# Record scatters three deep instead of two, shared rows prefetched one a step, and the last additions moved to GpSimd

## The chip, the cores and the metric

The kernel runs on one core of one Trainium2 chip. The metric is the device time of one execution in microseconds (us). Engines are named as the profile names them: PE (TensorE), DVE (VectorE), ACT (ScalarE), POOL (GpSimd) and SP (SyncE, which here only issues DMAs).

## What is computed

A transformer block in float32 on x of shape (4, 1024, 256): a cross attention of 16 heads against 64 context rows per batch, then a mixture of 8 experts with 2 of them chosen for each token, and one shared expert that every token passes.

```python
x = x + xattn(layernorm(x), ctx_768, Wq, Wk, Wv, Wo, bo)      # 16 heads of 64, softmax over 64 keys
xf = layernorm(x).reshape(-1, 256)                            # 4096 tokens
scores = softmax(xf @ gate_w.T); _, idx = top_k(scores + gate_b, 2)
w = take_along_axis(scores, idx)                              # 2 of 8 experts per token
expert(x) = silu((x @ w1 + b1) * (x @ w3 + b3)) @ w2 + b2     # 256 -> 352 -> 256
y = sum over the two chosen experts of w * expert_e(xf)
x = x + y + shared_expert(xf)
```

## The kernel before

The 4096 tokens are 32 tiles of 128 (NT = 32). After a setup of some 67 us the work runs in two phases, both software pipelined: in each step every engine works on another tile, and the order on an engine is the order of the code. All waits are semaphores written by hand.

**Attention phase**, `tile_step(s)`, s = 0 to 37. Tile t is loaded as `xin` at s = t-3 (SP, L445), its statistics are taken by DVE at s = t-2 (L999), and its scores, softmax and output follow on PE, ACT, DVE and POOL. At t+4 its sum with the residual `x2` is stored to `acc0` in DRAM (L453), at t+5 the normalised rows `xn2` to `xn2_scratch` (L449). DVE also chooses experts for tiles 0 to 7 and 8 to 15 in steps 14 to 19 and 22 to 27. In between SP loads the expert weights (L488 to L495). At step 20 SP also loads eight tiles of `xn2` rows (`shared_x`, L516) that the next phase begins with.

**Record scatters.** Each token gets, for each of its two experts, a slot in a table in DRAM (`slots_scratch`), where tokens of one expert stand together. POOL writes the table with 64 indirect DMAs (`scatter_record`, L649), two per tile, one record of 8 bytes for each of 128 tokens. Each waits for an earlier one by semaphore: `scat_out[k]`, k being the first or the second choice, so a scatter waits for the one two back. 22 of the 64 are issued during steps 20 to 30, one tile a step; the other 42 come behind the attention phase.

**Expert phase**, `unit_step(s)`, s = 0 to 106. It walks 103 units of 128 rows: shared tiles 0 to 19, then 71 routed units (`NU`) whose rows POOL gathers by the table (`gather`, L698) and whose results it adds into `acc0` or `acc1` (`scatter_add`, L705), then shared tiles 20 to 31. In step s PE does the second product of unit s-4 (`Y`), transposes the rows of s and the hidden values of s-3 (L1391, L1399) and does the first product of s-1. DVE computes low parts (`uxTl` L1124, `hTl` L1129), adds the bias (`uv` L1142) and multiplies (`hid<-uv` L1145); ACT copies out of PSUM and does silu. Before the first gather SP waits for all record scatters (L537) and then loads one piece of the table for each unit (L532), and POOL waits for that piece.

**The end.** Results of shared tiles 20 to 31 (units 91 to 102) go from PSUM to `zrow` (ACT, L897). When all scatter-adds have landed, SP loads both accumulators into `sums` in eight quads of four tiles (L551). DVE adds the two halves of one quad in each of the last eight steps, and `zrow` to the last three quads, between its other work (L1155, L1158, L1161); SP stores each quad (L555):

```python
both = [sums[:, i, q, :, :].rearrange("p a d -> p (a d)") for i in range(2)]
dve.wait_ge(sums_in[q], 32)
```

## Time and profile before

| | |
|---|---|
| time, median of 3 runs | 759.71 us (757.81 to 766.28) |
| the profiled execution's own time | 761.5 us |
| its span in the trace | 759.8 us |
| PE busy | 681.3 us, 90% of the span |
| DVE busy | 531.0 us, 70% |
| POOL busy | 409.8 us, 54% |
| ACT busy | 402.2 us, 53% |
| mean granted PE clock | 0.961 of full |

Busy time is a sum over stages with different limits, so it does not say what an edit is worth: that is read from the waits and from the stretch in which the edit lies. All times in the text are us from the start of the span.

### The profile page before, as it was taken

The numbers are of one execution on the slowest core, as the hardware profiler recorded it, in microseconds if no ns is written. First come the engines' busy times: TensorE is split into PE (matmuls) and PEld (weight loads), VectorE is DVE, ScalarE is ACT, GpSimd is POOL, SyncE is SP. The second block draws the span as 40 slices with busy tenths as digits, with TensorE's granted clock in tenths as the row PEclk, the third lists the DMA queues.
The fourth block names the chain that finished last, engine by engine and source line by source line (L and its number), as shares of the span: only waits on it lengthen the run. The fifth ranks groups of instructions, "written<-read, shape, count | busy, mean of one in ns | idle before, by whom it ended". The sixth has DMA issues, their size and how long they took to land.

```text
span 759.8 us, 16832 instructions
## 1 busy us (share of the span) xinstructions
PE 681.3 (90%) x4645; PEld 636.6 (84%) x4646; DVE 531.0 (70%) x1085; ACT 402.2 (53%) x1311; POOL 409.8 (54%) x506
## 2 busy tenths in 40 slices
PE   4997799999998999967899079999999999999995
PEld 3775599998897889857899079999999999999994
DVE  4766688788976887658889036666666666666677
ACT  3875778787766667746533024434443444344342
POOL 5343475544566677433454435777677777766200
PEclk9989999999999999988999679999999999999998
DMA  8201222235436664316221024454444444455495
GB/s 240 77 0 42 91 70 78 84 109 162 131 93 151 122 122 92 101 59 177 67 64 34 2 64 63 74 72 74 76 72 69 76 74 71 70 96 105 94 392 229
DMA packets 71508, 74.83 MB, mean 98 GB/s; under 512 B 21130, under 2 KB 65012, under 8 KB 71444
## 3 DMA queue, kind: packets, MB, share of 16 engines
q1 hardware_dynamic: 51940, 50.51, 24.3%
q0 software_dynamic: 15760, 18.96, 15.3%
q10 hardware_dynamic: 3744, 4.59, 1.7%
q8 instruction: 30, 0.49, 0.3%
q14 instruction: 34, 0.28, 0.2%
HBM read 47.22 MB, written 26.81 MB: 97 GB/s over the span
## 4 chain that ended last, share of the span: by engine, by line
PE 74%; DMA 13%; DVE 5%; issue 4%; ACT 2%; POOL 2%; SPq 1%; ACTq 0%; POOLq 0%; DVEq 0%
PE ps L1221 61%; DMA slots_scratch<-record,slot 11%; PE ps L1399 4%; PE ps L1318 3%; PE ps L1391 2%; PE ps L1295 1%; DMA wq_sb<-in_L_xattn_Wq 1%; PE ps L1308 1%; POOL slots_scratch L649 1%; ACT prob L763 1%; DMA xin<-in_x 1%; DVE hmax L1008 1%; SPq L516 1%; PE ps L1346 1%; DVE sums L1158 0%
## 5 line engine op out<-in xcount | busy, mean ns | idle before, releaser
L705 POOL DMA_INDIRECT acc_scratch<-yrow,slots x71 | 112.0, 1578 | 71.0 <-ACT yrow L889 70.7
L889 ACT ACTIVATE yrow<-ps,slots 128x256 f32<-128x256 f32 x71 | 33.7, 475 | 148.2 <-PE ps L1221 131.4
L1221 PE MATMUL ps<-AU,xTh 128*128 128x512 f32 x256 | 96.9, 423 | 9.1 <-DVE xTl L1021 9.1
L1221 PE MATMUL ps<-AU,pTh 128*128 128x256 f32 x512 | 100.2, 288 | 0.0
L1221 PE MATMUL ps<-w13h,uxTh 128*128 x284 | 97.7, 344 | 0.0
L1142 DVE TENSOR_TENSOR uv<-ps,b 128x704 f32<-128x704 f32 x71 | 63.3, 892 | 47.7 <-PE ps L1221 46.5
L649 POOL DMA_INDIRECT slots_scratch<-record,slot x64 | 66.1, 1033 | 56.2 <-DMA slots_scratch<-record,slot 46.8
L1221 PE MATMUL ps<-w13h,uxTl 128*128 x284 | 91.6, 322 | 0.0
L1221 PE MATMUL ps<-w13l,uxTh 128*128 x284 | 91.2, 321 | 0.0
L1124 DVE TENSOR_TENSOR uxTl<-ps,uxTh 128x256 fp32r<-128x256 f32 x103 | 43.6, 423 | 65.7 <-ACT uxTh L903 65.3
L698 POOL DMA_INDIRECT xrow<-xn_scratch,slots x71 | 69.8, 983 | 26.0 <-issue 20.1
L1221 PEld LDWEIGHTS ps<-AU,pTh 128*128 128x128 f32 x512 | 81.4, 189 | 0.0
L763 ACT ACTIVATE prob<-ps,nmax 128x64 f32<-128x64 f32 x256 | 76.3, 338 | 6.0 <-DVE nmax L1011 6.0
L1221 PE MATMUL ps<-AU,pTl 128*128 128x256 f32 x256 | 72.2, 282 | 0.0
L604 POOL TENSOR_TENSOR prob<-prob,hinv 128x1024 f32<-128x1024 f32 x32 | 60.9, 1904 | 20.5 <-DVE hinv L990 20.4
L1221 PEld LDWEIGHTS ps<-AU,xTh 128*128 128x128 f32 x256 | 49.8, 195 | 19.1 <-DVE xTl L1021 10.1
L1391 PE MATMUL ps<-ident,xrow 128*128 128x128 f32 x206 | 40.5, 279 | 26.5 <-DMA xrow<-xn_scratch,slots 22.9
L1221 PE MATMUL ps<-w2h,hTh 128*128 x213 | 63.0, 296 | 0.0
L1221 PE MATMUL ps<-w2l,hTh 128*128 x213 | 60.4, 283 | 0.0
L1221 PE MATMUL ps<-w2h,hTl 128*128 x213 | 60.1, 282 | 0.0
L763 ACT ACTIVATION_READ_ACCUMULATOR prob<-ps,nmax 128x1 f32 x256 | 59.3, 232 | 0.0
L1129 DVE TENSOR_TENSOR hTl<-ps,hTh 128x384 fp32r<-128x384 f32 x103 | 57.3, 556 | 0.3 <-ACT hTh L908 0.3
(237 smaller groups left out, 2009.9 us busy)
## 6 DMA issues: line engine op xcount, KB each, us to landing
sums<-acc_scratch SPq DMA_DIRECT2D x16, 512.0 KB, 10.9
w_raw<-in_L_ffn_w SPq DMA_DIRECT2D x16, 352.0 KB, 4.0
xin<-in_x SPq DMA_DIRECT2D x32, 128.0 KB
xres<-in_x SPq DMA_DIRECT2D x32, 128.0 KB
acc_scratch<-x SPq DMA_DIRECT2D x32, 128.0 KB
xn_scratch<-xn SPq DMA_DIRECT2D x32, 128.0 KB
xrow<-xn_scratch SPq DMA_DIRECT2D x32, 128.0 KB
out_x<-sums SPq DMA_DIRECT2D x8, 512.0 KB, 2.8
```

The source lines that it names most:

```text
L604: pool.tensor_tensor(heads, heads, hinv[:, p, :].unsqueeze(2).to_broadcast([P, HEADS, NK]), ALU.mult).then_inc(norm_ok, 1)
L649: pool.indirect_dma_start(slots_dram, bass.IndirectOffsetOnAxis(ap=slot[:, k, t:t + 1], axis=0), record[:, t, k, :], None).then_inc(scat_o ...
L698: pool.indirect_dma_start(xrow[:, m, :], None, xn2_dram, bass.IndirectOffsetOnAxis(ap=slots[:, u, 0:1], axis=0)).then_inc(gather_in[m], 16)
L705: pool.indirect_dma_start(acc_dram[u % 2], bass.IndirectOffsetOnAxis(ap=slots[:, u, 0:1], axis=0), yrow[:, m % YRING, :], None, compute_op ...
L763: act.activation(prob[:, p, h * NK:(h + 1) * NK], ps[:, s_bank(p) + h // 8, h % 8 * NK:(h % 8 + 1) * NK], ACT.Exp, bias=nmax[:, p, h - HS: ...
L889: act.activation(yrow[:, y, :], ps[:, 6 + m % 2, 0:D], ACT.Copy, scale=slots[:, bass.ds(u, 1), 1].bitcast(F32)).then_inc(y_ok, 1)
L1124: dve.tensor_tensor(uxTl[:, p, :], ps[:, 0, 0:D], f32(uxTh[:, p, :]), ALU.subtract).then_inc(uxTl_ok, 1)
L1129: dve.tensor_tensor(hTl[:, :], ps[:, 5, 0:H3], f32(hTh[:, :]), ALU.subtract).then_inc(hTl_ok, 1)
L1142: dve.tensor_tensor(uv[:, :, :], ps[:, 1 + 2 * p:3 + 2 * p, 0:H], bias, ALU.add).then_inc(bias_ok, 1)
L1221: last = pe.matmul(out, stationary(k, a), moving(k, b), start=(k == 0 and i == 0), stop=(k == n - 1 and i == len(PARTS) - 1 and not more))
L1391: last = pe.transpose(ps[:, 0, k * P:(k + 1) * P], xrow[:, m, k * P:(k + 1) * P], ident[:, :])
L1399: last = pe.transpose(ps[:, 5, k * P:(k + 1) * P], hid[:, p, k * P:(k + 1) * P], ident[:, :])
```

## The change

It has five parts. (1) The 64 record scatters use three semaphores in turn (`FLIGHT = 3`): scatter n waits for n-3 and no more for n-2. SP waits for all three. Two semaphores more are needed for this and for the new end; they come from `raw2_in`, which now counts two experts on one semaphore, so that ACT's first copy of a pair waits for both. (2) The eight loads of shared rows leave step 20 and stand one each in steps 24 to 31, behind the expert weights of the step. (3) POOL, behind its last scatter-add, adds the two halves of all eight quads; DVE's eight additions of this kind go. (4) DVE adds `zrow` to quads 5 and 6 in steps 102 and 103. (5) For the last quad (units 99 to 102) ACT copies nothing out; in steps 103 to 106 DVE adds each tile's PSUM result to `sums` directly, ahead of its other work of the step, and SP stores it tile by tile.

```diff
--- before.py
+++ after.py
@@ -50,10 +50,12 @@
     NU = TOP * NT + E - 1
     RING = 8
     YRING = 4
+    FLIGHT = 3
     QUAD = 4
     NA = 20
     NB = NT - NA
     R0, R1 = NA, NA + NU
+    RD = R1 + NB - QUAD
     GROUPS = ((0, 8), (8, 16))
     REST = (16, NT)
     NREST = NT - 16
@@ -329,11 +331,11 @@
         rank_copied = sem("rank_copied")
         empty_raw = sem("empty_raw")
         empty_ok = sem("empty_ok")
-        scat_out = [sem(f"scat_out{k}") for k in range(TOP)]
+        scat_out = [sem(f"scat_out{i}") for i in range(FLIGHT)]
         slots_in = [sem(f"slots_in{i}") for i in range(RING)]
 
         raw13_in = [sem(f"raw13_in{e}") for e in range(E)]
-        raw2_in = [sem(f"raw2_in{e}") for e in range(E)]
+        raw2_in = [sem(f"raw2_in{i}") for i in range(E // 2)]
         w13_hi = sem("w13_hi")
         w2_hi = sem("w2_hi")
         w_lo = sem("w_lo")
@@ -358,8 +360,9 @@
         shared_row_out = [sem(f"shared_row_out{i}") for i in range(YRING)]
         z_row_ok = sem("z_row_ok")
         sums_in = [sem(f"sums_in{q}") for q in range(NT // QUAD)]
-        sums_ok = sem("sums_ok")
+        both_ok = sem("both_ok")
         out_ok = sem("out_ok")
+        last_ok = sem("last_ok")
         all_out = sem("all_out")
         y_out = sems("y_out")
         NALL = NT + NU
@@ -490,9 +493,9 @@
 
             def load_w2(e):
                 sp.wait_ge(pad2_zero, 1 if e < EARLY2 else 2)
-                sp.dma_start(w2_raw[:, e, 0:KH - 1, :], w2[e, 0:(KH - 1) * P, :].rearrange("(c p) d -> p c d", p=P)).then_inc(raw2_in[e], 16)
-                sp.dma_start(w2_raw[0:HR, e, KH - 1, :], w2[e, (KH - 1) * P:H, :]).then_inc(raw2_in[e], 16)
-                sp.dma_start(w2_raw[HR:HR + 1, e, KH - 1, :], b2[e, :].rearrange("(a d) -> a d", a=1)).then_inc(raw2_in[e], 16)
+                sp.dma_start(w2_raw[:, e, 0:KH - 1, :], w2[e, 0:(KH - 1) * P, :].rearrange("(c p) d -> p c d", p=P)).then_inc(raw2_in[e // 2], 16)
+                sp.dma_start(w2_raw[0:HR, e, KH - 1, :], w2[e, (KH - 1) * P:H, :]).then_inc(raw2_in[e // 2], 16)
+                sp.dma_start(w2_raw[HR:HR + 1, e, KH - 1, :], b2[e, :].rearrange("(a d) -> a d", a=1)).then_inc(raw2_in[e // 2], 16)
 
             def begin_step(s, par):
                 tile_step(s, par)
@@ -504,11 +507,10 @@
                     load_w2(s - 24)
                 if s in (31, 32):
                     load_w2(s - 25)
-                if s == 20:
+                if 24 <= s < 24 + RING:
                     for half in xn2_out:
                         sp.wait_ge(half, 16 * RING // 2)
-                    for t in range(RING):
-                        shared_x(t)
+                    shared_x(s - 24)
 
             def shared_x(t):
                 m, i = t % RING, shared_tile(t)
@@ -534,8 +536,8 @@
             for t in range(RING, NA):
                 shared_x(t)
             sp.wait_ge(eid_ok, 1)
-            for half in scat_out:
-                sp.wait_ge(half, 16 * NT)
+            for i in range(FLIGHT):
+                sp.wait_ge(scat_out[i], 16 * len(range(i, TOP * NT, FLIGHT)))
             for u in range(NU):
                 unit_slots(u)
             for t in range(R1, NALL):
@@ -549,11 +551,17 @@
                 b, j = divmod(q * QUAD, TPB)
                 for i in range(2):
                     sp.dma_start(sums[:, i, q, :, :], acc_tiles[i][:, b, j:j + QUAD, :]).then_inc(sums_in[q], 16)
-            for q in range(NT // QUAD):
+            for q in range(NT // QUAD - 1):
                 b, j = divmod(q * QUAD, TPB)
-                sp.wait_ge(out_ok, q + 1)
+                if q < NA // QUAD:
+                    sp.wait_ge(both_ok, q + 1)
+                else:
+                    sp.wait_ge(out_ok, q - NA // QUAD + 1)
                 sp.dma_start(out_tiles[:, b, j:j + QUAD, :], sums[:, 0, q, :, :]).then_inc(all_out, 16)
-            sp.wait_ge(all_out, 16 * (NT // QUAD))
+            for i in range(QUAD):
+                sp.wait_ge(last_ok, i + 1)
+                sp.dma_start(out_tiles[:, B - 1, TPB - QUAD + i, :], sums[:, 0, NT // QUAD - 1, i, :]).then_inc(all_out, 16)
+            sp.wait_ge(all_out, 16 * (NT // QUAD - 1 + QUAD))
 
 
         @block.gpsimd
@@ -645,9 +653,10 @@
                 return done
 
             def scatter_record(t, k):
-                wait(pool, scat_out[k], 16 * t)
+                n = TOP * t + k
+                wait(pool, scat_out[n % FLIGHT], 16 * (n // FLIGHT))
                 pool.indirect_dma_start(slots_dram, bass.IndirectOffsetOnAxis(ap=slot[:, k, t:t + 1], axis=0),
-                                        record[:, t, k, :], None).then_inc(scat_out[k], 16)
+                                        record[:, t, k, :], None).then_inc(scat_out[n % FLIGHT], 16)
 
             def begin_step(s, par):
                 tile_step(s, par)
@@ -714,6 +723,10 @@
                 scatter_add(u)
                 if u + ahead < NU:
                     gather(u + ahead)
+            for q in range(NT // QUAD):
+                both = [sums[:, i, q, :, :].rearrange("p a d -> p (a d)") for i in range(2)]
+                pool.wait_ge(sums_in[q], 32)
+                pool.tensor_tensor(both[0], both[0], both[1], ALU.add).then_inc(both_ok, 1)
 
 
         @block.scalar
@@ -858,7 +871,7 @@
                     act.activation(w13h[:, e, k, :], w13_raw[:, e, k, :], ACT.Copy).then_inc(w13_hi, 1)
 
             def high2(e):
-                act.wait_ge(raw2_in[e], 48)
+                act.wait_ge(raw2_in[e // 2], 96)
                 flat = [a[:, e, :, :].rearrange("p c d -> p (c d)") for a in (w2h, w2_raw)]
                 act.activation(flat[0], flat[1], ACT.Copy).then_inc(w2_hi, 1)
 
@@ -892,7 +905,7 @@
                         wait(act, Y_ok, t + 1)
                         wait(act, shared_row_out[y], 16 * (t // YRING))
                         act.activation(yrow[:, y, :], ps[:, 6 + m % 2, 0:D], ACT.Copy).then_inc(shared_row_ok, 1)
-                    else:
+                    elif t < RD:
                         wait(act, Y_ok, t + 1)
                         act.activation(zrow[:, t - R1, :], ps[:, 6 + m % 2, 0:D], ACT.Copy).then_inc(z_row_ok, 1)
                 t = s
@@ -1116,6 +1129,12 @@
             steps(NT, 2, 6, begin_step, begun=0)
 
             def unit_step(s, m, routed=None):
+                t = s - 4
+                if isinstance(t, int) and t >= RD:
+                    row = sums[:, 0, NT // QUAD - 1, t - RD, :]
+                    dve.wait_ge(both_ok, NT // QUAD)
+                    dve.wait_ge(Y_ok, t + 1)
+                    dve.tensor_tensor(row, ps[:, 6 + m % 2, 0:D], row, ALU.add).then_inc(last_ok, 1)
                 t = s
                 if has(t, NALL):
                     p = m % 2
@@ -1147,19 +1166,14 @@
                     low2(s - 5)
                 if isinstance(s, int) and 5 + E <= s < 5 + E + E - 3:
                     low13(s - 5 - E + 3)
-                q = s - NALL - LAG + NT // QUAD if isinstance(s, int) else -1
-                if q >= 0:
-                    both = [sums[:, i, q, :, :].rearrange("p a d -> p (a d)") for i in range(2)]
-                    dve.wait_ge(sums_in[q], 32)
-                    if q < NA // QUAD:
-                        dve.tensor_tensor(both[0], both[0], both[1], ALU.add).then_inc(out_ok, 1)
-                    else:
-                        z0 = (q - NA // QUAD) * QUAD
-                        dve.tensor_tensor(both[0], both[0], both[1], ALU.add).then_inc(sums_ok, 1)
-                        dve.wait_ge(sums_ok, q - NA // QUAD + 1)
-                        dve.wait_ge(z_row_ok, z0 + QUAD)
-                        dve.tensor_tensor(both[0], both[0], zrow[:, z0:z0 + QUAD, :].rearrange("p a d -> p (a d)"),
-                                          ALU.add).then_inc(out_ok, 1)
+                q = s - NALL + NT // QUAD - 2 if isinstance(s, int) else -1
+                if NA // QUAD <= q < NT // QUAD - 1:
+                    z0 = (q - NA // QUAD) * QUAD
+                    row = sums[:, 0, q, :, :].rearrange("p a d -> p (a d)")
+                    dve.wait_ge(both_ok, q + 1)
+                    dve.wait_ge(z_row_ok, z0 + QUAD)
+                    dve.tensor_tensor(row, row, zrow[:, z0:z0 + QUAD, :].rearrange("p a d -> p (a d)"),
+                                      ALU.add).then_inc(out_ok, 1)
 
             dve.wait_ge(lg_ok, NT)
             dve.wait_ge(O_ok, NT)
@@ -1374,8 +1388,10 @@
                         wait(pe, y_ok, t - 1 - R0)
                     elif t < R0 + 2:
                         wait(pe, shared_row_ok, t - 1)
+                    elif t < RD + 2:
+                        wait(pe, z_row_ok, t - 1 - R1)
                     else:
-                        wait(pe, z_row_ok, t - 1 - R1)
+                        wait(pe, last_ok, t - 1 - RD)
                     w2s = (w2h, w2l) if is_routed(t, routed) else (ws2h, ws2l)
                     product(ps[:, 6 + p, 0:D],
                             lambda k, part: (hTh, hTl)[part][:, k * P:(k + 1) * P],
```

SP's queue in the program's step 20, before: behind the loads of `xrow` stand the tile load of step 21 and all that follows.

```order
L516 DMA xrow<-xn_scratch 128x256 [waits xn2_out_odd,xn2_out_even]
L516 DMA xrow<-xn_scratch 128x256 x7
L445 DMA xin<-in_x 128x256 [waits xn_ok]
L449 DMA xn_scratch<-xn 128x256 [waits xn2_ok]
L453 DMA acc_scratch<-x 128x256 [waits x2_ok]
L457 DMA xres<-in_x 128x256 [waits x2_ok]
L488 DMA w_raw<-in_L_ffn_w 128x2x352 [waits O_ok]
L489 DMA w_raw<-in_L_ffn_w 128x2x352
```

SP's queue now in step 24, at the first of the eight places where one such load stands.

```order
L496 DMA w_raw<-in_L_ffn_w 128x2x256 [waits pad2_zero]
L497 DMA w_raw<-in_L_ffn_w 96x256
L498 DMA w_raw<-in_L_ffn_b 1x256
L518 DMA xrow<-xn_scratch 128x256 [waits xn2_out_odd,xn2_out_even]
L448 DMA xin<-in_x 128x256 [waits xn_ok]
L452 DMA xn_scratch<-xn 128x256 [waits xn2_ok]
L456 DMA acc_scratch<-x 128x256 [waits x2_ok]
L460 DMA xres<-in_x 128x256 [waits x2_ok]
```

The eight loads in a row are gone from the place ahead of `xin`, and one stands behind the three weight loads `w2` in each of steps 24 to 31 (from step 30 on partly without such loads). 

POOL's queue behind the attention phase, before: scatters of the fifth to the seventh tile left over.

```order
L649 DMA slots_scratch<-record,slot 33792x2 [waits scat_out0]
L649 DMA slots_scratch<-record,slot 33792x2 [waits scat_out1]
L649 DMA slots_scratch<-record,slot 33792x2 [waits scat_out0,slot_ok]
L649 DMA slots_scratch<-record,slot 33792x2 [waits scat_out1]
L649 DMA slots_scratch<-record,slot 33792x2 [waits scat_out0]
```

The same place now.

```order
L658 DMA slots_scratch<-record,slot 33792x2 [waits scat_out0]
L658 DMA slots_scratch<-record,slot 33792x2 [waits scat_out1]
L658 DMA slots_scratch<-record,slot 33792x2 [waits scat_out2,slot_ok]
L658 DMA slots_scratch<-record,slot 33792x2 [waits scat_out0]
L658 DMA slots_scratch<-record,slot 33792x2 [waits scat_out1]
```

The instructions are the same in number and order; only the semaphore that each waits on differs, with period three.

DVE's queue over the last steps, before (from step 103).

```order
L1129 TENSOR_TENSOR hTl<-ps,hTh 128x384 [waits Y_ok,hTh_ok]
L1142 TENSOR_TENSOR uv<-ps,bs 128x704 [waits z_ok,UV_ok]
L1145 TENSOR_TENSOR hid<-uv 128x352 [waits H_ok,bias_ok]
L1155 TENSOR_TENSOR sums<-sums 128x1024 [waits sums_in4]
L1129 TENSOR_TENSOR hTl<-ps,hTh 128x384 [waits Y_ok,hTh_ok]
L1158 TENSOR_TENSOR sums<-sums 128x1024 [waits sums_in5]
L1161 TENSOR_TENSOR sums<-sums,zrow 128x1024 [waits z_row_ok,sums_ok]
L1129 TENSOR_TENSOR hTl<-ps,hTh 128x384 [waits Y_ok,hTh_ok]
L1158 TENSOR_TENSOR sums<-sums 128x1024 [waits sums_in6]
L1161 TENSOR_TENSOR sums<-sums,zrow 128x1024 [waits z_row_ok,sums_ok]
L1158 TENSOR_TENSOR sums<-sums 128x1024 [waits sums_in7]
L1161 TENSOR_TENSOR sums<-sums,zrow 128x1024 [waits z_row_ok,sums_ok]
```

And now (from the end of step 102).

```order
L1175 TENSOR_TENSOR sums<-sums,zrow 128x1024 [waits z_row_ok,both_ok]
L1137 TENSOR_TENSOR sums<-ps,sums 128x256 [waits Y_ok,both_ok]
L1148 TENSOR_TENSOR hTl<-ps,hTh 128x384 [waits Y_ok,hTh_ok]
L1161 TENSOR_TENSOR uv<-ps,bs 128x704 [waits z_ok,UV_ok]
L1164 TENSOR_TENSOR hid<-uv 128x352 [waits H_ok,bias_ok]
L1175 TENSOR_TENSOR sums<-sums,zrow 128x1024 [waits z_row_ok,both_ok]
L1137 TENSOR_TENSOR sums<-ps,sums 128x256 [waits Y_ok,both_ok]
L1148 TENSOR_TENSOR hTl<-ps,hTh 128x384 [waits Y_ok,hTh_ok]
L1137 TENSOR_TENSOR sums<-ps,sums 128x256 [waits Y_ok,both_ok]
L1148 TENSOR_TENSOR hTl<-ps,hTh 128x384 [waits Y_ok,hTh_ok]
L1137 TENSOR_TENSOR sums<-ps,sums 128x256 [waits Y_ok,both_ok]
```

Behind each `hid<-uv` or `hTl` stood one or two additions of 1024 columns; two of these are left, and four additions of 256 columns out of PSUM have come, each ahead of the `hTl` of its step and each with a wait for `both_ok`, POOL's count.

## Rows read from the trace of the kernel before

**Rows 1.** The page, part 4: the chain that ended last.
```profile
PE ps L1221 61%; DMA slots_scratch<-record,slot 11%; PE ps L1399 4%; PE ps L1318 3%; PE ps L1391 2%; PE ps L1295 1%; DMA wq_sb<-in_L_xattn_Wq 1%; PE ps L1308 1%; POOL slots_scratch L649 1%; ACT prob L763 1%; DMA xin<-in_x 1%; DVE hmax L1008 1%; SPq L516 1%; PE ps L1346 1%; DVE sums L1158 0%
```

**Rows 2.** Waits of POOL, 330 to 440 us: total, times, longest.
```profile
POOL slots_scratch L649 <- DMA slots_scratch<-record,slot: 46.8, 29, 3.3
```

**Rows 3.** Timeline of POOL: start, duration, idle before and its releaser.
```profile
340.56 1.66 POOL L649 DMA_INDIRECT slots_scratch<-record,slot  x1 [0.41 <-issue]
...
415.46 0.96 POOL L649 DMA_INDIRECT slots_scratch<-record,slot  x1 [2.72 <-DMA slots_scratch<-record,slot]
...
419.00 0.96 POOL L649 DMA_INDIRECT slots_scratch<-record,slot  x1 [1.22 <-DMA slots_scratch<-record,slot]
...
433.98 0.96 POOL L649 DMA_INDIRECT slots_scratch<-record,slot  x1 [1.25 <-DMA slots_scratch<-record,slot]
439.40 0.99 POOL L698 DMA_INDIRECT xrow<-xn_scratch,slots  x1 [4.47 <-DMA slots<-slots_scratch]
```

**Rows 4.** Timeline of PE around its long wait.
```profile
442.55 0.69 PE L1391 MATMUL ps<-ident,xrow 128*128 128x128 f32 x2 [22.87 <-DMA xrow<-xn_scratch,slots]
...
448.59 0.38 PE L1391 MATMUL ps<-ident,xrow 128*128 128x128 f32 x2
...
452.12 0.38 PE L1391 MATMUL ps<-ident,xrow 128*128 128x128 f32 x2
```

**Rows 5.** Windows: busy time by engine, then PEclk, DMA share, GB/s.
```profile
340.00:360.00 20.00, 14.78 (x90) 13.42 (x89) 17.02 (x46) 11.37 (x21) 7.59 (x8) 0.78 0.61 173
434.00:445.00 11.00, 2.45 (x10) 2.46 (x11) 0.98 (x2) 1.26 (x3) 5.12 (x6) 0.50 0.20 43
```

**Rows 6.** Timeline of SP's DMA issues, steps 20 to 23.
```profile
220.64 4.96 SPq L516 DMA_DIRECT2D xrow<-xn_scratch  x8
225.65 0.43 SPq L445 DMA_DIRECT2D xin<-in_x  x1
...
227.00 0.32 SPq L453 DMA_DIRECT2D acc_scratch<-x  x1
...
246.38 0.33 SPq L453 DMA_DIRECT2D acc_scratch<-x  x1
...
254.38 0.33 SPq L453 DMA_DIRECT2D acc_scratch<-x  x1
```

**Rows 7.** Timeline of DVE in the step behind those issues.
```profile
231.27 0.43 DVE L999 BATCH_NORM_STATS2 st<-xin 128x6 f32<-128x256 f32 x1 [2.74 <-DMA xin<-in_x]
...
233.06 1.64 DVE L1011 TENSOR_SCALAR nmax<-hmax 128x8 f32<-128x8 f32 x1
...
250.62 0.30 DVE L1011 TENSOR_SCALAR nmax<-hmax 128x8 f32<-128x8 f32 x1
```

**Rows 8.** Timeline of POOL at the same two places.
```profile
233.27 1.40 POOL L660 MEMSET w_raw<- 128x1536 f32 x1
...
248.99 1.91 POOL L604 TENSOR_TENSOR prob<-prob,hinv 128x1024 f32<-128x1024 f32 x1 [0.70 <-DVE hinv L990]
```

**Rows 9.** POOL groups by shape: count, busy, mean ns.
```profile
L617 POOL TENSOR_TENSOR wol<-wo_raw,woh 128x256 fp32r<-128x256 f32 x8 | 5.8, 728 | 0.0
...
L671 POOL TENSOR_TENSOR ws2l<-ws,ws2h 128x768 fp32r<-128x768 f32 x1 | 1.8, 1844 | 0.0
```

**Rows 10.** The tile sums: first and last issue of a line; landing times.
```profile
L551 SPq DMA_DIRECT2D sums<-acc_scratch x16: 319/530/1052, 717.4 to 726.6; - x16
...
DMA to landing us min/median/max: 2.6/8.9/16.5
```

**Rows 11.** Timeline of DVE at the end.
```profile
745.02 0.55 DVE L1129 TENSOR_TENSOR hTl<-ps,hTh 128x384 fp32r<-128x384 f32 x1
...
746.93 0.52 DVE L1145 TENSOR_TENSOR hid<-uv 128x352 f32<-128x352 f32 x1
...
755.48 1.23 DVE L1161 TENSOR_TENSOR sums<-sums,zrow 128x1024 f32<-128x1024 f32 x1
```

**Rows 12.** Timeline of PE at the end.
```profile
753.03 0.28 PE L1221 MATMUL ps<-ws2l,hTh 128*128 128x256 f32 x1
```

## Prediction

> **What bounds the kernel now.** I read the page's chain first: which instructions the end followed from. 61% of it are PE's products at L1221, and the next entry by far is no engine's work but the landing of record scatters, 11% [rows 1]. PE's products are not touched by the change; the scatters are. So the second view is who waits for them. POOL waited 46.8 us in 29 of its 41 starts between 330 and 440 us for a scatter to land [rows 2]. That alone is no loss, POOL may have nothing else to do. The third view shows that it is one: PE stands idle for 22.87 us, from 419.68 to 442.55, until the first gathered rows land [rows 4], and these come from a table that is complete only when the last scatter has landed. So between 340 and 442 us two chains run beside each other, PE's twenty shared units and POOL's 42 scatters, and the scatters are later by 22.87 us.
>
> Two smaller places lie on the path too. In the attention phase DVE waits 2.74 us for a tile load that stood behind eight loads in SP's queue [rows 6, 7]. At the end DVE works on additions until 756.71 while PE's last product was done at 753.31 [rows 11, 12].
>
> **The change part by part.** The sum is made against the profiled execution's own 761.5 us; it lies 1.8 above the median of the runs, 759.71, so the predicted median is that much lower than the sum.
>
> (1) *Scatters three deep.* The first of the 42 starts at 340.56, the last at 433.98: 93.42 us for 41 gaps, 2.28 each [rows 3]. A scatter keeps POOL for 0.96 and 0.30 pass to the next, so 1.26 is the floor. From the last start to the first gather are 5.42 us (landing, SP's load of a table piece, its landing), and from there to PE 3.15 [rows 3, 4]: 8.57 in all, and the change leaves them as they are. PE is free at 419.68, so its idle time is gone once the last scatter starts at 411.11 or before, that is at 1.72 us per gap.
>
> What will a gap be? If a scatter with three under way lands as soon as with two, two thirds of the time are needed where landings set the pace, 1.52, and more where the floor does. I replayed the 42 starts with each one's own time to landing, each start the later of "1.26 behind the one before" and "when the one three back has landed": the last starts at 408.9, 1.67 per gap, and PE's idle time is gone with 2 us to spare. The other bound is that the table's writes have a rate of their own which more of them under way do not raise: then 2.28 stay and the gain is nothing. Rows bear on which is nearer. The pace follows the other traffic: between 415.46 and 433.98 ten gaps take 1.85 each, while the mean is 2.28 and the first twenty microseconds, where the DMA engines are 61% busy, are slower still [rows 3, 5]. And the last scatter, alone under way, has landed and let SP and a second DMA follow within 5.42, against 3.54 for the landing of one of a pair (415.46 to 419.00, [rows 3]); one alone is therefore not much quicker than two, which speaks for a delay and not for a rate. Some rise with a third is likely. With all landings 10% later the same replay gives 413.7 (1.78 per gap), with 20% 419.3, with 30% 425.1, with 50% 436.7. I take 10%, nearest to the rows: the last start at 413.7, PE resumes at 422.3 and has stood for 2.6 us. Gain 22.9 - 2.6 = 20.3.
>
> To this comes PE's clock. It was granted 0.50 from 434 to 445 [rows 5], the lower of its two levels, 1.2 GHz, behind the long idle time; the first step after it took 6.04, from 442.55 to 448.59, the next one 3.53 [rows 4]. With 2.6 us of idle time I expect it to stay up: gain 2.5, or nothing if it falls again.
>
> The two experts on one `raw2_in` semaphore cost nothing: the last of these loads is issued in step 32 of the attention phase, and ACT asks for that pair in step 4 of the next phase, eight steps later. SP and POOL wait for three counts in place of two: nothing, they are complete together.
>
> (2) *One shared row load a step.* The eight issues take SP from 220.64 to 225.60; the tile load queued behind them starts at 225.65 and DVE has it at 231.27, after 2.74 us of standing [rows 6, 7]. By SP's stores the two steps from 227.00 to 246.38 last 19.38, and the one after them 8.00 [rows 6], so without the delay both would be 16. Of the excess of 3.4 the 2.74 go for certain; behind them DVE was also caught by POOL's memset (below), which may come again. I take 3.4, between 2.7 and 4.2, the upper end if the two steps are a little shorter than their neighbour, in which experts are chosen. New, one issue of 0.5 us and 128 KB stand behind the weight loads in eight steps; SP has several us free in each, and the next tile load is needed a step later. Its cover is that slack; if it were gone, each load would cost its 0.5, 4 us in eight steps.
>
> (3) to (5) *The end.* POOL has no row of an addition of 2 x 1024 columns. By its subtractions of 256 and 768 columns, 0.728 and 1.844 us, a column costs 2.18 ns, which gives 2.40 for 1024 [rows 9]; its multiplication of 1024 with one repeated operand is 1.91 [rows 8]. I take 2.40, since both operands are full here. The last quad's halves are issued by 726.6 and land 16.5 later, 743.1 [rows 10]. The issues begin at 717.4, so the eight quads land within 25.7 us, some three apart; POOL keeps pace and ends its eighth addition at 743.1 + 0.3 + 2.4 = 745.8. DVE first asks for it in step 103, where it starts `hTl` at 745.02 [rows 11]. It now stands until 745.8, adds 256 columns out of PSUM (some 0.4, by 0.55 for the 384 of `hTl`) and starts `hTl` 1.2 later; half of that is given back in the next two steps, which lost two and three additions of 1.22. PE's last product ends 0.8 later than 753.31, at 754.1, and only one small addition follows, to 754.6, in place of 756.71 [rows 11, 12]: a gain of 2.1. The last store is a quarter as large; I count nothing for that.
>
> Against this stands what DVE and POOL do to each other. DVE's `nmax` at 233.06 took 1.64 us and ended with POOL's memset at 234.67; at 250.62 it took 0.30 and ended, at 250.92, with POOL's multiplication (248.99 and 1.91) [rows 7, 8]. So a DVE instruction of this kind stands until POOL's is over. The additions would meet `hid<-uv` and the two `zrow` additions, which have both operands in SBUF. If these stand in the same way, a `hid<-uv` of 0.52 [rows 11] meets an addition of 2.4 in nearly every step and stands for half of that on average, and POOL loses the 0.52 in turn; walked through over the last ten steps, that puts PE's last product 2.2 later than without it, and the gain is gone. I take 0.8, nearer to the second.
> By the Trainium skill (SBUF — State Buffer, Who interferes with whom) a VectorE instruction with two SBUF inputs contends with a GpSimd instruction that reads SBUF, and the second to issue blocks fully until the first is done; that is what speaks against part (3). The trace agrees for `nmax`, which ended with POOL's instruction both times; no row shows it for two inputs from SBUF against a GpSimd addition. By this rule the end's term would be 0 in place of 0.8, and by its absence 2.1.
>
> Sum: 20.3 + 2.5 + 3.4 + 0.8 = 27.0. 761.5 - 27.0 = 734.5, as a median 732.7, say 733.
>
> **The rivals.** *The writes have a rate of their own in part.* Landings 15 to 40% later leave PE idle for 5 to 20 us, probably with the slow clock behind it. For it: a pair's gaps are 1.85 where nothing else runs, well above 1.26, and the two scatters of a tile write neighbouring slots. Against it: the quiet stretch is faster than the busy one. At 25% the last start is near 422, the gain 12 + 0 + 3.4 + 0.8, the median 743.5; the span of this case is 736 to 751.
> *The rate is all.* The gap stays 2.28, and parts (2) to (5) alone remain: 761.5 - 1.8 - 4.2 = 755.5.
> *Slower than before.* Three scatters under way hinder each other so that a gap is longer than 2.28. In the replay this needs landings 45% later; since the other parts give 4.2, it decides from 53%. At 70% the last start is at 448, 14 us later than before: 759.7 + 14 - 4.2 = 769.5. The 1.85 in the quiet stretch with two under way, where a single one takes more than 2, speaks against it.
> *The end goes without mutual waits.* Then the end gives 2.1, and with landings unchanged part (1) gives all of 22.9 + 2.5, part (2) up to 4.2: 759.7 - 31.7 = 728.
> *The change does not do what it says* for part (2): if the loads delay the tile load of each following step by their 0.5, 4 us come back, 737.
>
> **How the numbers follow.** Forecast, 729.5 to 736: 0.56. Partly a rate, 736 to 751: 0.25. Wholly a rate, near 755: 0.07. Slower: 0.02. Better than forecast, 726 to 729.5: 0.10. The range 725 to 749 leaves out the last two cases of loss and the upper end of the second, 0.13. About 1%, 7.6 us, is what a measurement of this kernel can tell from no change; faster by more than that holds below 752.1, 0.90; slower above 767.3, 0.02; between them 0.08.
>
> **What would show it.** PE's wait for the first gathered rows falls from 22.87 to under 5; the last scatter starts 68 to 75 us after the first of the 42, not 93; POOL's waits for scatters fall from 46.8 to some 20; the clock stays up there. SP's stores in steps 21 to 23 are 7.5 to 8.5 apart and DVE has no wait for `xin`. POOL's eight additions take 2.4 each, and `hid<-uv` beside them is longer than 0.52 if the two engines exclude each other. I am wrong if the gap per scatter stays above 1.9: then the gain is under 18.

## The result, and the profile after

The median fell from 761.04 us (757.81 to 766.28, 4 runs) to 742.85 us (739.84 to 749.38, 4 runs): a ratio of 0.974, 95% interval 0.969 to 0.979. In a second session the changed kernel took 739.47 (736.25 to 743.47, 6 runs), again 0.974 (0.969 to 0.979). The forecast was 733 with a range of 725 to 749. The time lies inside the range, but the gain is some 18 to 22 us and not 27. Ratios and intervals, here and below, leave out the slow runs (more than 1.5% above the fastest of the same kernel: 2 of 6 with four scatters in flight, 4 of 6 with six), medians are of all runs.

The profiled execution took 745.34, its span 743.6. Part 4 of its page, the chain that ended last:

```profile
PE ps L1235 62%; DMA slots_scratch<-record,slot 8%; PE ps L1415 4%; PE ps L1332 3%; PE ps L1407 3%; POOL slots_scratch L658 2%; DMA xin<-in_x 1%; PE ps L1309 1%; DMA wq_sb<-in_L_xattn_Wq 1%; PE ps L1322 1%; ACT prob L776 1%; DVE hmax L1021 1%; PE ps L1360 1%; DVE st L1056 0%; DVE x L1054 0%
```

The landings are still second in it: 8%, where they were 11% [rows 1]. POOL's waits between 320 and 440 us (total, times, longest):

```profile
POOL slots_scratch L658 <- DMA slots_scratch<-record,slot: 29.5, 18, 5.4
```

They were 46.8 in 29 [rows 2]. POOL's timeline, the first of the 42 scatters, the longest wait, the last scatter and the first gather:

```profile
337.29 1.66 POOL L658 DMA_INDIRECT slots_scratch<-record,slot  x1 [0.41 <-issue]
...
389.85 1.28 POOL L658 DMA_INDIRECT slots_scratch<-record,slot  x1 [5.41 <-DMA slots_scratch<-record,slot]
...
418.36 0.96 POOL L658 DMA_INDIRECT slots_scratch<-record,slot  x1 [0.30 <-issue]
424.02 0.99 POOL L707 DMA_INDIRECT xrow<-xn_scratch,slots  x1 [4.70 <-DMA slots<-slots_scratch]
```

41 gaps take 81.07 us, 1.98 each, against 93.42 and 2.28 [rows 3] and a forecast of 1.78. PE's timeline at the first routed unit:

```profile
427.18 0.69 PE L1407 MATMUL ps<-ident,xrow 128*128 128x128 f32 x2 [7.77 <-DMA xrow<-xn_scratch,slots]
...
433.47 0.39 PE L1407 MATMUL ps<-ident,xrow 128*128 128x128 f32 x2
```

PE stands for 7.77 us in place of 22.87, and the step behind takes 6.29, so the clock still fell (6.04 in [rows 4]). Windows around it (span, busy time and count by engine, PEclk, DMA share, GB/s):

```profile
418.00:428.00 10.00, 2.23 (x16) 2.03 (x15) 1.42 (x2) 0.49 (x2) 3.92 (x5) 0.74 0.13 27
428.00:434.00 6.00, 6.00 (x30) 6.00 (x28) 2.36 (x4) 1.49 (x5) 2.84 (x3) 0.57 0.42 111
```

In the attention phase the burst of eight loads is gone, but DVE's wait for `xin` is not. It comes a step later, behind two weight loads in SP's queue (SP's issues; DVE's wait):

```profile
230.33 0.45 SPq L491 DMA_DIRECT2D w_raw<-in_L_ffn_w  x1
230.82 0.47 SPq L492 DMA_DIRECT2D w_raw<-in_L_ffn_w  x1
```

```profile
236.12 0.43 DVE L1012 BATCH_NORM_STATS2 st<-xin 128x6 f32<-128x256 f32 x1 [4.19 <-DMA xin<-in_x]
```

At the end POOL adds and DVE stands beside it (POOL's and DVE's timelines):

```profile
709.01 2.40 POOL L729 TENSOR_TENSOR sums<-sums 128x1024 f32<-128x1024 f32 x1 [10.43 <-DMA sums<-acc_scratch]
...
720.86 2.38 POOL L729 TENSOR_TENSOR sums<-sums 128x1024 f32<-128x1024 f32 x1 [0.66 <-DMA sums<-acc_scratch]
```

```profile
710.32 1.47 DVE L1164 TENSOR_TENSOR hid<-uv 128x352 f32<-128x352 f32 x1
...
717.41 0.52 DVE L1164 TENSOR_TENSOR hid<-uv 128x352 f32<-128x352 f32 x1
720.95 2.67 DVE L1164 TENSOR_TENSOR hid<-uv 128x352 f32<-128x352 f32 x1
```

An addition takes 2.40, as forecast. `hid<-uv` is 0.52 when it meets no addition, and otherwise stands until the addition is over: 710.32 + 1.47 = 711.79 against POOL's end at 711.41.

Where the 16.2 us of span between the two profiled executions went: PE's wait 15.1 less; the end (first load of the sums to the end of the span) 41.1 in place of 42.3, 1.2 less; 4.7 less ahead of the first scatter, where no code changed. Against these, 1.4 more from the first scatter to the first of the 42, 3.0 more in PE's twenty shared units beside them (82.1 against 79.1), and 0.4 more from there to the sums.

### The profile page after: what moved, and what is told of

Read it like the earlier page. It is cut to its first block, busy times and chain, and to the rows that moved or that the text cites. A ratio compares the mean times of both kernels' runs of the same rounds, so it can differ in the third digit from the quotient of the medians.

```text
span 743.6 us, 16844 instructions
## 1 busy us (share of the span) xinstructions
PE 676.8 (91%) x4645; PEld 632.3 (85%) x4646; DVE 527.4 (71%) x1080; ACT 402.4 (54%) x1307; POOL 431.5 (58%) x514
## 4 chain that ended last, share of the span: by engine, by line
PE 75%; DMA 11%; issue 4%; DVE 4%; POOL 3%; ACT 2%; SPq 0%; ACTq 0%; POOLq 0%; DVEq 0%
PE ps L1235 62%; DMA slots_scratch<-record,slot 8%; PE ps L1415 4%; PE ps L1332 3%; PE ps L1407 3%; POOL slots_scratch L658 2%; DMA xin<-in_x 1%; PE ps L1309 1%; DMA wq_sb<-in_L_xattn_Wq 1%; PE ps L1322 1%; ACT prob L776 1%; DVE hmax L1021 1%; PE ps L1360 1%; DVE st L1056 0%; DVE x L1054 0%
## 5 line engine op out<-in xcount | busy, mean ns | idle before, releaser
L1164 DVE TENSOR_TENSOR hid<-uv 128x352 f32<-128x352 f32 x103 | 59.9, 581 | 3.5
## 6 DMA issues: line engine op xcount, KB each, us to landing
sums<-acc_scratch SPq DMA_DIRECT2D x16, 512.0 KB, 10.5
```

The source lines that it names most:

```text
L1164: dve.tensor_tensor(hid[:, p, 0:H], uv[:, 0, :], uv[:, 1, :], ALU.mult).then_inc(z_ok, 1)
```

## The experiments

Ratios are against runs of the kernel before on the same chip, whose medians were 761.0 to 761.4, 763.0 beside the pauses and 758.5 beside the last kernel. "In flight" is the most that may be under way. "42 to sums" is the stretch from the start of the first of the 42 scatters to SP's first load of the sums; it holds all that the scatters' pace can change.

| kernel | in flight | us per scatter | PE idle | 42 to sums | median us |
|---|---|---|---|---|---|
| before | 2 | 2.28 | 22.9 | 376.9 | 759.71 |
| scatters alone | 3 | 1.88 | 6.7 | 361.4 | 744.48 |
| rows alone | 2 | 2.27 | 23.0 | 376.3 | 758.29 |
| end alone | 2 | 2.28 | 22.9 | 375.8 | 759.08 |
| changed | 3 | 1.98 | 7.8 | 365.2 | 742.85 |
| changed, again | 3 | 1.81 | 2.6 | 358.1 | 739.47 |
| changed, one | 1 | 3.57 | 75.9 | 429.6 | 829.5, one run |
| changed, two | 2 | 2.29 | 23.4 | 377.6 | 758.16 |
| changed, four | 4 | 1.71 | 0 | 365.7 | 744.33 |
| changed, six | 6 | 1.44 | 0 | 380.0 | 764.54 |
| five, one pause | 5 | 1.68 | 0 | 351.4 | 738.22 |
| five, two pauses | 5 | 2.09 | 15.1 | 368.6 | 753.51 |
| rows 64 bytes apart | 2 | 1.70 | 0 | 351.2 | 729.3, one run |
| the same, timed | 2 | 1.67 | 0 | 351.2 | 731.76 |

### One part at a time

**Scatters alone.** The kernel before with

```
-        scat_out = [sem(f"scat_out{k}") for k in range(TOP)]
+        scat_out = [sem(f"scat_out{i}") for i in range(FLIGHT)]
...
-                wait(pool, scat_out[k], 16 * t)
+                n = TOP * t + k
+                wait(pool, scat_out[n % FLIGHT], 16 * (n // FLIGHT))
```

> The kernel before with the scatters alone changed (three in flight on three semaphores, the w2 loads of two experts on one semaphore to have one free). Theory A (the landings come about 20% later with three in flight, and the restart of PE ends last): the 42 scatters start within 79 to 82 us of the first, PE is idle some 7 to 9 us instead of 22.9, the clock falls after it as before, and the time is about 14 to 15 us under the kernel before. Rival B (the longer stretch of PE ahead of the last scatter, 82.1 us against 79.1, belongs to the scatters): then PE is idle 10 us or less but its own stretch from the first scatter is again near 82 us. If it is a stray of one execution, the stretch is back at 79 us and PE idles 3 us longer.

With it goes the pairing of the `raw2_in` semaphores. Measured: 0.979 (0.975 to 0.983), 16.1 us by the ratio. PE's shared stretch was 79.75, so the scatters alone do not lengthen it by 3.

**Rows alone.** The kernel before with

```
-                if s == 20:
+                if 24 <= s < 24 + RING:
...
-                    for t in range(RING):
-                        shared_x(t)
+                    shared_x(s - 24)
```

> The kernel before with the shared rows alone changed (one a step in steps 24 to 31). The prediction had 3.4 us for it. Theory A (the input rows of the next tile now wait behind the weight loads instead of behind the burst, and the reading of after had a gain of nothing from first scatter to the first of the 42, 125.5 us against 124.1): within 1 us of the kernel before. Rival B (the gain is there and was hidden in after by the scatters with their longer landings, which take part of the same DMA queues): 2.5 to 4 us faster, and 120 to 121.5 us between these two scatters.

Measured: 0.9967 (0.9935 to 0.9999), 2.5 us. From the first scatter to the first of the 42 it took 119.7 us against 124.1 in the kernel before. Rival B is nearer, though the interval of the time holds theory A as well; the traces part the two. Steps 21 to 23 (by SP's stores) take 27.4 us in the kernel before, 27.2 and 27.3 in the two other traces with its order of the rows, 23.9 here and 23.7 in the changed kernel with two in flight. With more in flight part of this gain is gone, though not in the order of depth: 26.2 and 25.2 with three, 25.6 with four, 24.2 with six. The first execution of the changed kernel (125.5) also had a second wait for `xin`, and its step 26 took 12.0; in its second (121.6) the same step took 9.2.

**The end alone.** `FLIGHT = 2` in the changed kernel, and the rows back in one burst at step 20.

> The changed kernel with two scatters in flight and the shared rows in one burst, so that of the change only the end is left (POOL adds the two accumulators, DVE adds the last four rows straight from PSUM, each stored by itself). Theory A (additions of POOL and DVE with both operands in SBUF stop each other, so DVE's small products of the end wait 0.5 to 2.1 us each): 41 us from the first load of the sums to the end against 42.35, and the time 1.0 to 1.4 us under the kernel before. Rival (the end is worth nothing, and the 1.2 us were the shorter drain of other queues): within 0.3 us.

Measured: 0.9986 (0.9957 to 1.0015), which alone would tell nothing. The trace tells it: 41.07 us from the first load of the sums to the end, against 42.34, 42.09 and 41.96 in the three traces with the old end, and 40.8 to 41.1 in all others with the new one but one (41.6). So 1.1 us.

**The changed kernel again**, in the same session.

> The changed kernel once more, beside its parts on the same chip. Theory: the parts add up, 14 to 15 us for the scatters, 0 to 1 for the rows, 1.2 for the end: 16 to 18 us under the kernel before. If PE's stretch from the first of the 42 scatters to its idle time is 79 us this time, the 3 us of the first execution were a stray and PE idles 10 to 11 us; if 82 us again, the change causes it.

Measured: 19.9 us by the ratio; the parts give 16.1 + 2.5 + 1.1 = 19.7. They add up. This execution (span 737.0) is the one that the forecast drew: 1.81 us per scatter, PE idle for 2.56. Still its span is 4.2 us above the forecast's (734.5 - 1.7 = 732.8). Its PE timeline shows half of that, DVE's what DVE saw of it, and a window the clock (busy time by engine, PEclk, DMA share, GB/s):

```profile
421.96 0.44 PE L1407 MATMUL ps<-ident,xrow 128*128 128x128 f32 x2 [2.56 <-DMA xrow<-xn_scratch,slots]
...
425.55 0.38 PE L1407 MATMUL ps<-ident,xrow 128*128 128x128 f32 x2
...
429.81 0.39 PE L1235 MATMUL ps<-ws2h,hTh 128*128 128x256 f32 x1 [1.63 <-DVE hTl L1148]
430.98 0.39 PE L1407 MATMUL ps<-ident,xrow 128*128 128x128 f32 x2
```

```profile
427.51 0.89 DVE L1161 TENSOR_TENSOR uv<-ps,bs 128x704 f32<-128x704 f32 x1 [3.66 <-remote]
```

```profile
425.50:431.00 5.50, 3.87 (x29) 3.59 (x29) 3.36 (x6) 1.54 (x4) 0.73 (x1) 1.00 0.28 73
```

("<-remote": a count ended the wait, but no instruction of the trace that gives such a count had ended shortly before it.) PE's first step takes 3.59 at a granted clock of 1.00, 2.45 less than the 6.04 in the kernel before, so the clock did stay up. But the next one takes 5.43, and not for the clock, which reads 1.00 there too: PE is busy for 3.87 of 5.50 us and stands 1.63 for DVE's `hTl`, which came late because DVE had stood 3.66. Both steps take 9.02, against 9.57 in the kernel before. The other half is PE's shared stretch, 81.4 in place of 79.1, again with a DVE wait "<-remote" of 2.5, up to 370.3, and a PE step of 5.5, from 369.1; the first execution has the same at the same place.

### How deep

The only edit in these four is the number in `FLIGHT = 3`.

> The changed kernel with two scatters in flight in place of three (rows and end as changed). Theory A (the stall of about 2 us at 30 to 33 us behind the first of the 42 scatters, with DVE and ACT both released late, is brought by deeper scatters in this code): gone here, PE's stretch from the first of the 42 scatters to its idle time is 79 us. Rival B (it hangs on where the changed program's instructions lie, not on the scatters): it stays, 81 to 82 us. Both: gap per scatter 2.25 to 2.3 us, PE idle 20 to 23 us, and the time 3 to 4 us under the kernel before (rows 2.5, end 1.1).

> The changed kernel with four scatters in flight. Theory A (a landing is mostly a delay, which queued neighbours lengthen a little, about 3 to 3.5 us alone, 4 to 5 with two in flight, 5 to 6 with three): the gap falls to 1.5 to 1.65 us, the last of the 42 starts 62 to 68 us after the first, PE does not wait for the first gather, and the time is 3 to 5 us under that of three in flight, 735 to 738. Rival B (landings are a rate from three in flight on): the gap stays at 1.8 to 2.0 and the time at 739 to 742.

> The changed kernel with six scatters in flight. Theory A: the gap is 1.3 to 1.45 us, near the 1.26 us that a scatter takes on POOL when it waits for nothing, PE waits no more than with four, and the time is the same as with four within 1 us. Rival B (a rate): the gap stays at 1.8 to 2.0. Rival C (full queues of small writes hold up the shared rows and the products' stores): PE's stretch from the first of the 42 scatters grows past 84 us.

> The changed kernel with one scatter in flight: each waits for the one before, so the gap is a scatter's time on POOL, its landing and 0.26 us. Theory A (a delay of 3.2 us alone): a gap of 3.2 to 4.2 us, the last of the 42 starts 130 to 170 us after the first. Rival B (a rate of one landing in 1.9 to 2.2 us whatever is in flight): a gap of 2.3 us as with two.

With two the stretch is 78.9 and no step of PE in it is stalled; the time is 0.997 (0.993 to 1.001) of the kernel before. Theory A holds for the gaps: 3.57, 2.28, 1.8 to 2.0, 1.71, 1.44, so deeper is always quicker for POOL. It fails for the time. With four it is 0.977 (0.970 to 0.984), no better than with three. With six the kernel takes about as long as before: 764.54, but the six executions lie between 748.5 and 771.3, too far apart for a ratio. Each of them is slower than every one of the changed kernel's six in its second session (736.25 to 743.47), although the last scatter starts 34 us sooner than before: rival C, with a stretch of 107.3. Between 338 and 430 us of the run with six, who waited for what:

```profile
PE ps L1235 <- issue: 25.0, 4, 16.3
POOL xrow L707 <- PE ps L1407: 22.8, 3, 18.0
ACT yrow L907 <- remote: 22.7, 3, 12.3
```

and its timelines of PE and of ACT:

```profile
364.79 0.38 PE L1407 MATMUL ps<-ident,xrow 128*128 128x128 f32 x2
365.01 0.49 PE L1415 MATMUL ps<-ident,hid 128*128 128x128 f32 x3
...
383.71 0.58 PE L1235 MATMUL ps<-ws2h,hTh 128*128 128x256 f32 x1 [16.30 <-issue]
385.80 0.63 PE L1407 MATMUL ps<-ident,xrow 128*128 128x128 f32 x2
```

```profile
374.82 0.38 ACT L907 ACTIVATE yrow<-ps 128x256 f32<-128x256 f32 x1 [12.35 <-remote]
...
382.58 0.49 ACT L921 ACTIVATE hTh<-ps 128x384 fp32r<-128x384 f32 x1 [5.24 <-remote]
```

One step of 3.5 us takes 21.0, another 10.9. POOL runs through this without a wait until 383, a scatter every 1.26 us. SP issues a load of rows 0.4 us after PE's transposes of a tile (359.90 after 359.49); the one that belongs to 364.79 it issues at 376.9, after 16.7 us of "<-remote". ACT's `yrow` at 374.82 asks for a product recorded before 364.95, while DVE at 367.74 already used one that PE made after it. `yrow` also waits for a store to land; `hTh` waits for PE alone, for that product and for the transposes at 365.01, and starts at 382.58. So it is not the work that is late but its count. The rows' queues carry next to nothing in the meantime. DMA queues between 364 and 382 us (packets, MB, share of 16 engines), with six:

```profile
q1 hardware_dynamic: 84, 0.08, 9.7%
q0 software_dynamic: 400, 0.01, 1.8%
```

and in the kernel before:

```profile
q1 hardware_dynamic: 719, 0.65, 16.9%
q10 hardware_dynamic: 720, 0.66, 10.5%
q0 software_dynamic: 288, 0.01, 1.3%
```

The rows' loads (q1) and stores (q10) follow PE, so their absence is a result as much as a sign. In the run with four, steps of 5.5 and 10.5 us (366.9 and 401.5) stand beside rows of scatters some 1.3 apart. The stalls of 2 us in the changed kernel's two traces have the same look. That they are the same thing is not shown.

### An even beat

POOL clears a tile that is free there between two scatters, so that they cannot come in bursts:

```
+            def pause(i):
+                for c, n in enumerate(PAUSE):
+                    wait(pool, paused, i * len(PAUSE) + c)
+                    pool.memset(slots.rearrange("p u c -> p (u c)")[:, 0:n], 0).then_inc(paused, 1)
```

> The changed kernel with five scatters in flight and, between two of the 42, one memset of POOL on a tile that is free there (128x142, about 0.2 us by the shapes of the trace, and some 0.1 us until POOL sees it done), so that scatters go out in an even beat of about 1.6 us and not in bursts of 1.26. Theory A (what starves the rows' loads and stores in the runs with four and six in flight is a row of scatters back to back, with never a moment in which none is queued; a beat slower than the 1.27 us at which they are served leaves moments): the last of the 42 starts 64 to 68 us after the first, PE waits neither for rows nor for the first gather beyond 1 us, its stretch stays at 79 us, and the time is 734 to 738, 3 to 6 us under three in flight. Rival B (it is the number queued that matters): steps of 5 us and more in the stretch, time 742 or more.

> As the run before, with two memsets in a row (128x142 and 128x64), a beat of about 1.8 to 1.9 us. Theory A: an even beat, no step of PE above 5.4 us in the stretch, the last scatter 74 to 78 us after the first, PE idle 3 to 6 us before the first routed tile, time 737 to 741, as three in flight or a little under. Rival B as for the run before.

One pause: 0.9675 (0.9615 to 0.9735). Up to five are in flight, and a landing takes 6.1 us, the median between 364 and 382, while a scatter starts every 1.6: nearly four on average. Yet every step of PE in the stretch is as in the kernel before (from 372.9 on 3.5 to 4.2), and PE goes from the shared to the routed units without a gap. The mean pace is that of the run with four (1.68 against 1.71), where steps of up to 10.5 stood. So it is not the number under way or the mean pace that stalls the others, as far as two traces can tell; theory A holds for the steps, the last scatter (69.1 us after the first) and the median (738.2) lie just beyond its bounds, and 42 to sums is 25.5 us shorter than before. POOL's timeline shows the beat:

```profile
373.44 0.23 POOL L666 MEMSET slots<- 128x142 int32 x1
373.94 0.97 POOL L660 DMA_INDIRECT slots_scratch<-record,slot  x1 [0.28 <-POOL slots L666]
374.91 0.23 POOL L666 MEMSET slots<- 128x142 int32 x1
375.42 0.97 POOL L660 DMA_INDIRECT slots_scratch<-record,slot  x1 [0.28 <-POOL slots L666]
```

Two pauses cost more than I had worked out: POOL never waits for a landing, but a scatter with both memsets takes at least 1.98 us and 2.09 on average, in place of 1.8 to 1.9. PE idles 15.1: 0.988 (0.984 to 0.993). No step was stalled in it either.

### Records 64 bytes apart

The changed kernel with `FLIGHT = 2` and a table whose rows lie 64 bytes apart. A scatter still writes 8 bytes a row.

```
-    slots_dram = nc.dram_tensor("slots_scratch", [BLOCKS * P, 2], I32, kind="Internal").ap()
+    slots_dram = nc.dram_tensor("slots_scratch", [BLOCKS * P, 16], I32, kind="Internal").ap()
...
-                    dve.tensor_copy(slot[:, :, a:b], v[:, 4:6, :]).then_inc(slot_ok, 1)
+                    dve.tensor_scalar(slot[:, :, a:b], v[:, 4:6, :], 8.0, None, ALU.mult).then_inc(slot_ok, 1)
...
-                pool.indirect_dma_start(slots_dram, bass.IndirectOffsetOnAxis(ap=slot[:, k, t:t + 1], axis=0),
+                pool.indirect_dma_start(slots_dram.rearrange("r (a c) -> (r a) c", c=2), bass.IndirectOffsetOnAxis(ap=slot[:, k, t:t + 1], axis=0),
```

Its initial fill is eight transfers of the same source tile, since the contents repeat.

> The changed kernel with two scatters in flight (the same code took 2.27 to 2.29 us a scatter in all four traces of it) and a table whose rows lie 64 bytes apart in place of 8: each scatter still writes 8 bytes a row. Theory C (the landing is long because neighbouring 8-byte writes meet in the same stretch of memory): the gap falls to 2.0 or less. Rival D (the delay is of the queue and its descriptors, not of the memory): 2.2 to 2.35 as before.

> The kernel of the run before once more (two scatters in flight, table rows 64 bytes apart, the shared rows and the end as in the changed kernel), now timed against the kernel before. Theory C (neighbouring 8-byte writes made the landings long, and held up the loads of the attention phase as well): gap 1.65 to 1.85 us, PE not idle before the first routed tile, 118 to 122 us from the first scatter to the first of the 42, and a median of 727 to 734, 4 per cent under the kernel before. If the single execution was a stray, the gap is back near 2.28 and the time at 755 or more.

Measured at last: 731.76 (727.29 to 734.42, 6 runs), 0.9645 (0.9604 to 0.9685): with two in flight, some 7 us less than the changed kernel by the two ratios, and the lowest ratio of all, though its interval overlaps that of one pause. The gap went from 2.29 to 1.67. Between the two kernels stand only the row distance and what it needs: slots times 8, the fill in eight transfers, and table pieces read as 8 bytes of every 64. POOL's waits from 320 to 440 us in the timed kernel's trace, and its DMA queues and landings from 364 to 382 (the last row: count, median us from issue to landing):

```profile
POOL slots_scratch L660 <- DMA slots_scratch<-record,slot: 17.7, 15, 2.7
```

```profile
q1 hardware_dynamic: 720, 0.66, 13.5%
q10 hardware_dynamic: 720, 0.66, 10.5%
...
slots_scratch<-record,slot POOLq DMA_INDIRECT x11, 2.3
```

A landing takes 2.3 with up to two under way, and 2.2 over all 42. In the run with one in flight and records side by side it took 3.2 (median of 16, 340 to 420 us), alone; in the run with two pauses, where 2.3 were under way on average, 4.8. The other transfers of the stretch gain too: ACT's stores of `yrow` land in 2.4 us and SP's loads of `xrow` in 2.5, against 5.1 and 4.7 with two pauses. In the attention phase the wait for `xin` is gone in both traces: the step that had it takes 8.2 us, against 8.5 to 11.1 in the eight other traces with this order of the rows and two or more in flight, and the first scatter to the first of the 42 takes 118.1 in both, against 119.7 to 126.0. Theory C holds in that the row distance sets the landing. That records meet in one stretch of memory is not shown beyond this: 64 bytes is the only distance tried, and the table grew eightfold with it.

## Why the prediction was right, and where its sizes were not

- **The bound and the main mechanism**: right. With a third scatter under way POOL waits less, PE resumes sooner, and this is 16.1 of some 20 us.
- **"With all landings 10% later ... I take 10%"** is the term that was mis-sized. The three traces of three in flight have 1.81, 1.88 and 1.98 us per scatter in place of 1.78; by the same replay, landings 12 to 24% later. PE idled 2.6, 6.7 and 7.8, not 2.6. The other end of my bounds was wrong in kind: 2.28 for two is no rate of the queue (1.44 with six), and no plain delay either, since the delay itself hung on how the records lie.
- **The clock, 2.5**: right in mechanism, but rarely had. At 6.7 and 7.8 us of idle time it fell. At 2.6 it stayed up and the first step gave back 2.45; the next lost 1.9 of that again to a wait of DVE that the sum did not hold.
- **"Their cover" was never asked for PE's own stretch.** I let the scatters take nothing from PE's shared units. In two of three traces they took 2.3 and 3.0, and with six in flight more than the whole gain.
- **The rows, 3.4**: 2.5 (0.1 to 4.9) in the run of this part; its steps 21 to 23 were 3.5 shorter, as forecast, but 1.1 and 2.2 in the two executions of the changed kernel. The wait for `xin` moved behind the weight loads; it was gone only where records lay 64 bytes apart, and with one in flight, where the steps were longer anyway. That the loads would delay each next tile by 0.5 did not happen: steps 24 to 31, which issue them, take 62.2 to 62.8 us in the two runs with two in flight and the changed kernel's second execution, against 62.9 in the kernel before (65.5 in its first, with the step of 12.0).
- **The end, 0.8**: 1.1 to 1.3. The mutual stop of DVE and POOL was there as described; of the full 2.1 about half is left. The Trainium skill (SBUF — State Buffer, Who interferes with whom) says that a VectorE instruction with two SBUF inputs contends with a GpSimd instruction that reads SBUF, for ports that are an exclusive lock. The trace agrees for two operands in SBUF, 2.67 in place of 0.52 against an addition that ended 0.4 before. That this would cost the whole gain, as the prediction took from it, did not come true. Giving the additions to DVE, to price this apart, was not tried.
- **Of the rivals**, "partly a rate" named the time better (736 to 751) than the forecast's own 729.5 to 736, and by the gap it was the same case with another name; that the result lay in the range owes something to the range being wide enough for both. "Slower than before" was written for longer gaps; what makes it slow with six is the opposite, gaps that are too short.
- **Its own signs were missed** by the profiled execution: a gap of 1.98, above the 1.9 from which "I am wrong" was written, a wait of PE of 7.77 and not under 5, the last scatter 81.1 us after the first and not 68 to 75, and a wait for `xin`. The second execution met the first three (1.81, 2.56, 74.0).

What stays open: why counts come late while small neighbouring writes pile up. The Trainium skill (DMA: Bandwidth & Descriptors, Queues, rings and completion order) says that a DMA's increment lands only after every earlier write of its DMA engine. That would hold up transfers' counts; PE's counts to ACT and SP are not such, and no run here parts the two. Nor is it shown that the 5.43 us step behind the restart is the same thing. Bursts onto records 64 bytes apart with more than two in flight were not tried.

The traces themselves leave a rival open. The four of the pauses and of the rows 64 bytes apart come from chips 2 and 3, the others, where the chip is on record, from 1 and 13; and these four alone hold nearly every count. In the routed units (450 to 690 us), where the code is the same, the one with one pause has 798 of the 798 counts that the engines' instructions give, the changed kernel's 613 of 800. Of the 1024 counts of the scatters' landings these four have 1007 to 1022, the kernel before 889, three in flight 703 to 769, four 620 and six 456. So the traces without stalls were recorded more fully, and side-by-side records without pauses, two in flight or more, were not traced on those chips. That the bursts stall the engines, and not the recording or the chip, is argued: with two in flight no step was stalled on the chip of the runs with four and six. The ratios do not hang on this, since each is taken against the kernel before on the same chip.

## What to carry to other kernels

When a chain of small scatters sets the pace, look at where the records lie before you deepen it: 8-byte records 64 bytes apart gave with two in flight what side by side needed up to five and a pause for. A deeper queue must be checked at the engines that have nothing to do with it, by the lengths of their steps and by waits with no named releaser. And read two traces before a term of a few us is called gained or lost: the same code differed by 4 us in one stretch.

## What I had not expected of the hardware

- Side by side, a lone scatter of 128 records of 8 bytes lands in 3.2 us (median); 64 bytes apart, one of two lands in 2.3.
- While scatters went out every 1.26 us onto neighbouring records, up to six in flight, PE stood for 16.3 us, ACT for 12.3 and SP for 16.7, and POOL waited for nothing. Eight in a row without a wait onto records 64 bytes apart, at most two in flight (394.97 to 404.45 us in the single execution), stopped nobody.
- An idle time of PE of 2.56 us left the granted clock at 1.00 (first step 3.59); one of 6.7 let it fall (6.06).
